# Moving the own part of a token mix into the attention weights, and normalisations to GpSimd, in a one-core perceiver layer

## The reference, cut to what matters

```python
# 1: keys through a cosine of a second projection; softmax; values
K_hat = jnp.cos(jnp.einsum('bsd,dr->bsr', K, Wr) + br)
scores = jnp.einsum('bqr,bkr->bqk', Q, K_hat)
# 2: each token attends to the 8 most similar earlier tokens of its row
attn = jax.nn.softmax(score - row_max, axis=-1)
msg = jnp.einsum('bts,bsd->btd', attn, x)
blended = mix * x + (1.0 - mix) * msg
delta = jax.nn.gelu(blended * gain + bias, approximate=False) * scale
# 3: one of 8 experts (256 -> 1024 -> 256, Gelu) for each token
out = p_max * next_states
```

## Time and profile before

| | us |
|---|---|
| median of 3 runs | 482.03 (481.74 to 483.29) |
| the profiled execution, its own time | 479.15 |
| its span in the trace | 477.3 |

### The profile page before, as it was taken

One profiled execution on the slowest core, in us unless ns is written; L12 is line 12 of the kernel. 1 busy time (PEld: TensorE's weight loads), 2 busy tenths in 40 slices (PEclk: granted clock), 3 DMA queues, 4 the chain that ended last, 5 costly groups with the idle time before them and its releaser, 6 DMA issues. The chain is left out here.

```text
span 477.3 us, 10300 instructions
## 1 busy us (share of the span) xinstructions
PE 420.0 (88%) x3121; PEld 286.7 (60%) x3121; DVE 275.9 (58%) x856; ACT 257.5 (54%) x573; POOL 216.4 (45%) x358
## 2 busy tenths in 40 slices
PE   6767999999969969979877879968999999999992
PEld 6424454445425425434433456857999999999991
DVE  2536887989878868968969946755321221222220
ACT  1455777788847848848756755526232232332330
POOL 1663552765575566556646445364233232222110
PEclk9797999999999989989989989989999999999997
DMA  9996696896775766758776452455679546556100
GB/s 193 309 297 173 153 229 174 222 200 169 194 190 145 197 173 164 224 123 204 227 168 190 167 209 71 162 175 203 209 249 346 186 176 225 172 199 231 33 0 0
DMA packets 119433, 87.45 MB, mean 183 GB/s; under 512 B 78606, under 2 KB 109072, under 8 KB 119252
## 3 DMA queue, kind: packets, MB, share of 16 engines
q1 hardware_dynamic: 111828, 75.82, 56.8%
q0 software_dynamic: 3744, 9.46, 5.7%
q10 hardware_dynamic: 3808, 1.52, 1.5%
HBM read 79.15 MB, written 8.53 MB: 184 GB/s over the span
## 5 line engine op out<-in xcount | busy, mean ns | idle before, releaser
L1206 ACT ACTIVATE XF<-pT,b_now 128x128 f32<-128x128 f32 x184 | 52.2, 369 | 91.0 <-PE pT L1407 91.0
L1407 PEld LDWEIGHTS pT<-XF,stage 128*128 128x128 f32 x736 | 87.8, 195 | 3.9 <-issue 1.7
L1407 PE MATMUL pT<-XF,stage 128*128 128x128 f32 x736 | 89.4, 280 | 0.7 <-issue 0.4
L1420 PE MATMUL pK<-W,XF 128*128 x368 | 85.0, 381 | 2.8 <-ACT XF L1206 2.1
L1420 PEld LDWEIGHTS pK<-W,XF 128*128 128x128 f32 x368 | 67.5, 190 | 11.8 <-issue 3.7
L1382 PE MATMUL pK<-stage,Wkr 128*128 128x512 f32 x128 | 67.7, 656 | 0.0
L305 POOL TENSOR_SCALAR ve<-mv 128x1 f32<-128x1 f32 x48 | 10.9, 227 | 115.1 <-DVE mv L640 115.0
L1382 PE MATMUL pT<-stage,Wkr 128*128 128x512 f32 x128 | 61.6, 605 | 0.0
L1179 ACT ACTIVATE stage<-stage 128x512 f32<-128x512 f32 x64 | 38.7, 627 | 26.1 <-DVE stage L721 26.0
L721 DVE TENSOR_TENSOR stage<-stage 128x512 f32<-128x512 f32 x64 | 49.5, 774 | 0.8
L402 POOL DMA_INDIRECT out_dram<-XF,token_i x23 | 23.1, 1004 | 56.5 <-DVE XF L847 50.4
(11 more groups left out here) (190 smaller groups left out, 679.5 us busy)
## 6 DMA issues: line engine op xcount, KB each, us to landing
stage<-in_L_ffn_W_dram SPq DMA_DIRECT2D x23, 1024.0 KB, 5.1
stage<-in_ctx_dram SPq DMA_DIRECT2D x32, 512.0 KB, 5.1
XF<-in_ctx_dram SPq DMA_DIRECT2D x252, 64.0 KB, 2.3
W<-in_L_ffn_W_dram SPq DMA_DIRECT2D x8, 1024.0 KB, 6.1
rows_by_token<-rows_out SPq DMA_DIRECT2D x16, 256.5 KB
ctx_last<-in_ctx_dram SPq DMA_DIRECT2D x64, 32.0 KB, 4.5
X<-in_x_dram SPq DMA_DIRECT2D x1, 1792.0 KB, 12.6
tokens_by_expert<-no_token POOLq DMA_DIRECT2D x2, 576.0 KB, 8.1
```

The source lines that it names most:

```text
L1206: ins = act.activation(f_hT[b][:, n * P:(n + 1) * P], pT[i][:, (n % 4) * P:(n % 4 + 1) * P], ACT.Gelu, bias=b1_now[:, b, n:n + 1])
L1407: mm = pe.matmul(pT[i][:, (n % 4) * P:(n % 4 + 1) * P], W1[q][:, c, n * P:(n + 1) * P], f_inT[:, q % 2, c * P:(c + 1) * P], start=c == 0, ...
L1420: mm = pe.matmul(p_out, f_hT[q % 2][:, n * P:(n + 1) * P], W2[:, bass.ds(e, 1), n, :].rearrange("p o d -> p (o d)"), start=n == 0, stop=n ...
```

## The change

Own part: the matrix own_part, mix on the diagonal, is made once. A new GpSimd step `mix` forms (1 - mix) * att + own_part from the 128x32 weights, and this is transposed and multiplied with hm = h * gain + bias (rows of the weights sum to one, so the bias may stand inside). The product is blended * gain + bias itself: hg, y and VectorE's addition are gone, and ScalarE takes the Gelu from PSUM.

Normalisations: h and the normalised result are made by GpSimd. `rstd` also makes the negative mean, and the three normalisations are (x + minus_mean) * rstd.

Order: `xn_T` comes after `scores`, its output moves to bank b6; `h_T` comes after a second projection and `probs_T`; `scatter` is split in two in a step, one half in the middle and one at the end; the planning, the second projection's steps and the drain are in another order; the prologue starts with a projection, and the loads that aren't needed early (most of X, the empty token lists) go later. The new `p_rank` and one message use bank b4.

```diff
+        own_part = sb("own_part", [P, T])
...
-        p_xnT = b5[:, 0:D]
+        p_xnT = b6[:, 0:D]
...
-            def rstd(g, mv, ve, rs, mv_r, ve_r, rs_r):
...
+            def rstd(g, mv, ve, minus_mean, rs, i):
...
+                pool.tensor_scalar(minus_mean[:], mv[:, 0:1], -1.0, None, ALU.mult).then_inc(S[f"mean{i}_r"], 1)
...
+            def normal_h(g):
+                at_least(pool, S["hT_tr"], g - 1)
+                at_least(pool, S["hm_m"], g - 1)
+                pool.wait_ge(S["mean2_r"], g + 1)
+                pool.wait_ge(S["rs2_r"], g + 1)
+                pool.tensor_scalar(h[:, g % 2, :], group_of(X, g), minus_mean2[:, 0:1], rs2[:, 0:1], ALU.add, ALU.mult
+                                   ).then_inc(S["h_r"], 1)
...
+            def mix(g):
+                pool.wait_ge(S["att_r"], g + 1)
+                at_least(pool, S["attT_cp"], g)
+                pool.tensor_scalar(mixed[:], att[:], sc[:, 3:4], None, ALU.mult).then_inc(S["others_r"], 1)
+                pool.wait_ge(S["others_r"], g + 1)
+                pool.tensor_tensor(mixed[:], mixed[:], own_part[:], ALU.add).then_inc(S["mixed_r"], 1)
...
+            for s in range(1, NG):
                 if s >= 2:
                     rstd_h(s - 2)
                     base(s - 2)
...
+                    normal_h(s - 2)
+                if s == 3:
+                    own_parts()
+                if s >= 3:
+                    mix(s - 3)
+                last_key(s)
+                last_value(s - 1)
+                if s >= 2:
+                    messages(s - 2)
+                if s == NG - 1:
+                    gather(0)
+                if s >= 6:
+                    if s % 2 == 0:
+                        count_pair(s // 2 - 3)
+                        tokens_of(s // 2 - 3)
+                    else:
+                        scatter(s // 2 - 3, (0,) if s + 1 < NG else (0, 1))
                 if s >= 4:
                     rstd_out(s - 4)
...
+                    rstd_x(s + 1)
                     normal_x(s + 1)
                     add_bv(s + 1)
...
+                if s in (2, 3):
+                    no_tokens(s - 2)
+                if s >= 7 and s % 2 and s + 1 < NG:
+                    scatter(s // 2 - 3, (1,))
...
+            sp.wait_ge(S["ctxT_r"], 2)
+            load_by_feature(1, 1)
...
+            sp.dma_start(X[:, 2:4, :], x_v[:, 2:4, :]).then_inc(S["xnext_ld"], 16)
...
-                act.activation(gel[:], y[:], ACT.Gelu).then_inc(S["gelu_r"], 1)
+                act.activation(gel[:], p_msg[g], ACT.Gelu).then_inc(S["gelu_r"], 1)
...
             def xn_T(g):
                 pe.wait_ge(S["xn_r"], g + 1)
-                at_least(pe, S["selected"], g - 2)
-                at_least(pe, S["y_r"], g - 3)
...
+                at_least(pe, S["x1_r"], g - 1)
...
+            for s in range(1, NG):
                 ctx_project(s, 0, 0)
...
+                scores(s - 1)
                 if s >= 7 and s % 2:
                     pe.wait_ge(S["logits_r"], s - 4)
                     rank(s // 2 - 3)
+                xn_T(s)
+                ctx_project(s, 0, 1)
+                probs_T(s - 1)
                 if s >= 2:
                     h_T(s - 2)
...
+                ctx_project(s, 1, 0)
                 if s >= 2:
...
+                    similar(s - 2)
+                values(s - 1, max(0, (s - 5) // 2))
                 queries(s)
...
+                ctx_project(s, 1, 1)
                 if s >= 2:
                     small_scores(s - 2)
...
+                value_T(s - 1)
```

More of the change, by code:

```diff
@@ L213, in perceiver_layer @@
         p_scoreB = b5[:, 0:T]
-        p_msg = b5[:, 0:D]
+        p_msg = [(b4 if g == NG - 2 else b5)[:, 0:D] for g in range(NG)]
         p_hT = b6[:, 0:D]
@@ L364, in late_constants, with own_parts, tokens_of @@
                 made_at["masks"] = n[0]
-                pool.wait_ge(S["gains"], 2)
-            def scatter(q):
+            def own_parts():
+                made(pool.memset(own_part[:], 0.0))
+                for j in range(BG):
+                    keep(own_part[j * T:(j + 1) * T, :], [[-1, T]], 0, 1, ALU.not_equal, 1.0)
+                pool.wait_ge(S["scal_dve"], 3)
+                made(pool.tensor_scalar(own_part[:], own_part[:], sc[:, 2:3], None, ALU.mult))
+            def tokens_of(q):
                 r0, i = 2 * (q % 2), q % 2
@@ L454, in _ @@
                     add_bv(s + 1)
-                if s >= 2:
-                    self_part(s - 2)
-                if s == 0:
-                    late_constants()
-                if s == NG - 1:
-                    gather(0)
-                if s >= 7 and s % 2:
-                    scatter(s // 2 - 3)
+                if s in (2, 3):
+                    no_tokens(s - 2)
+                if s >= 7 and s % 2 and s + 1 < NG:
+                    scatter(s // 2 - 3, (1,))
+            base(14)
@@ L464, in _ @@
             rstd_h(14)
-            base(14)
-            self_part(14)
+            normal_h(14)
             last_value(15)
-            rstd_out(12)
             gather(1)
             count_pair(5)
+            mix(13)
+            tokens_of(5)
+            gather(2)
+            rstd_out(12)
+            scatter(5)
             rstd_h(15)
             base(15)
-            self_part(15)
-            gather(2)
+            normal_h(15)
+            mix(14)
+            messages(14)
+            rstd_out(13)
@@ L1129, in late_block @@
                 result(j, q, turn)
-            for j in range(4, EARLY):
-                begin(j + 1)
-                end(j)
             for j in range(EARLY, NBLK):
@@ L1250, in xn3T_copy @@
                 act.copy(xn3T[:].rearrange("p c n -> p (c n)"), p_xn3T).then_inc(S["xn3T_cp"], 1)
-            for s in range(NG):
-                xnT_copy(s)
+            turn(0, 0)
+            turn(0, 1)
+            xnT_copy(0)
+            sine(0, 0, 0)
+            sine(0, 0, 1)
+            turn(0, 2)
+            queries(0)
+            act.wait_ge(S["last_fr"], 1)
+            act.activation(khat_last[:], last_frac, ACT.Sin, scale=TWO_PI).then_inc(S["khat_last_r"], 1)
+            turn(0, 3)
+            sine(0, 0, 2)
+            sine(0, 0, 3)
+            for s in range(1, NG):
                 if s >= 3:
@@ L1561, in router @@
                 mm.then_inc(S["route_mm"], 1)
-            for s in range(NG):
-                if s == 0:
-                    last_transposes()
-                xn_T(s)
+            ctx_project(0, 0, 0)
+            ctx_project(0, 0, 1)
+            xn_T(0)
+            last_transposes()
+            ctx_project(0, 1, 0)
+            last_project()
+            small_transposes()
+            queries(0)
+            ctx_project(0, 1, 1)
+            for s in range(1, NG):
                 ctx_project(s, 0, 0)
-                if s == 0:
-                    last_project()
-                if s >= 1:
-                    scores(s - 1)
+                scores(s - 1)
                 if s >= 7 and s % 2:
```

596 lines of the change are left out of this document (301 added, 295 removed).

## The result

The changed kernel takes 447.34 us in the median of four runs (446.76 to 449.0), the kernel before, beside it, 482.66 (481.74 to 483.33): ratio 0.9275, 95% interval 0.9243 to 0.9306. The forecast was 445, with 434 to 461 as its range. The profiled execution took 447.48 us, 31.7 less than the 479.15 of before. The one of before lay 2.9 us under its median and this one doesn't, so the two profiles show some 3 us less of a gain than the medians do.

The account below looks back on a forecast made before the run. TensorE's work and gaps set the end (busy 420.0 of 477.3 us). Gains 5 + 0.7 + 21.6 + 9.5 = 36.8 take the profiled 479.15 to 442.4, the median from 482.03 to 445; range 434 to 461.

Parts of the forecast that it names:

- the drain: Loop's end to block 7's transposes: 77.0 us becomes 67.5, a gain of 9.5, between 3 and 13.
- steps 2 and 3: Second and third loop steps: gain their two short gaps, 0.7 us; X's load in step 2 could cost up to 2.
- the last blocks: Last 16 blocks, from block 7's transposes at 350.25: no TensorE idle time, 7.25 us each; the change touches nothing.
- the loop: Steps 4 to 15: 198.3 us becomes 176.7, 12 steps of 14.6 plus 1.5 for planning; gain 21.6.
- the prologue: Before step 2: group 1's second-half transpose starts at 30, not 35.66; gain 5 us, between 2 and 8.
- The stall, and h_T's place: Even steps from 8: 3.22 us stall and slow projection go; h at 5.0 us, `h_T` at 5.2 instead of 3.1.
- About 14.3 us of TensorE work: Ordinary loop step: 14.90 us stretch with one 0.6 gap; 14.3 of work plus 0.3 of small stalls gives 14.6.
- GpSimd's load: Per loop step: net +1.5 us, +2.8 at the upper price; 12 to 13.3 of 14.3 with `scatter`, so it fits.
- Rival A: GpSimd becomes the loop's bound at normalisations' upper price: step 15.9 us, loop 192, time 459; chance 0.15.
- Interference: More GpSimd instructions slow VectorE's 128x512 subtraction: 0.8 us a step taken, at most 1.7; VectorE then 12.8 of 14.3.
- Gelu from PSUM: ScalarE in each step: Gelu 0.416 before, no cost as work is the same size; if late, `similar` would wait.
- Rival C: Slower than now: bank b6 makes TensorE wait twice a step, 1.3 us each; step 18.5, time 491; chance 0.04.

Follow-up runs that it names:

- first profile: Profiled execution of the changed kernel as first measured, unedited, against the kernel before: 447.48 us, median 447.34, ratio 0.9275.
- its second: Profile from a repeat of the changed kernel, unedited: median 448.64 us over six runs, ratio 0.9284; this profile is 3.7 us longer than the first.

## Why the prediction was right, step by step

**The time: nearer than its parts.** The forecast was made for the profiled execution, 479.15 less 36.8, or 442.4, and moved up to 445 for the median. The profiled execution took 447.48, so the parts brought 32.1 of 36.8 us: the drain is 3.7 short, steps 2 and 3 0.9, the last blocks 0.8, and the loop and the prologue are 0.7 ahead. The median came within 2.3 us because the kernel before had been profiled 3 us under its median and the changed one was not; that much is luck.

**The stall, and h_T's place: right.** The 3.22 us and the slow projection came from `scatter` ahead of `rstd_h`: taking it away alone brought 15 us. In the changed kernel the stall is gone by h_T's later place and a shorter queue ahead of `rstd_h` together. Step 10 starts at 153.55; h is ready 4.0 us into it, where my layout had 5.0, and h_T comes 5.1 us into it, where it had 5.2. GpSimd had more free time than I gave it.

**The work in a step: mis-sized.** "About 14.3 us of TensorE work" was 13.97. I had taken a stretch of 14.90 us and subtracted the 0.6 that its one bracketed gap shows. But its matmuls are 14.18, so it holds 0.72 of idle time: another 0.11 lies ahead of h (92.74 to 92.85), too short for a bracket. And 14.18 is still 0.21 more than the path needs. Step 4, with the 0.6 gap alone, lasts 14.69 (74.92 to 89.61), so this gap costs 0.72. The experiment with `scatter` moved says the same: its steps have shown gaps of 0.2 to 0.4 each and last 14.7. A matmul's shown duration reaches over the start of the next, back to back (1.98 for a projection whose successor starts 1.92 later, 139.55 to 141.47); ahead of a gap this tail is work on the page and lost time on the path. With the 0.3 of "small stalls" that are not there either, the eleven steps are 6.9 us shorter than forecast.

**Step 15: missed.** I gave steps 13 to 15 1.5 us for planning on VectorE and nothing for a wait of GpSimd. Step 15 holds a gap of 4.63 us and 2 us of matmuls at the lower clock behind it. The row of TensorE's gap and the queue of GpSimd above show the cause; the diff showed it beforehand. `gather(0)` stood ahead of `scatter` and `rstd_out`, and I had costed only when its own rows would land, not what is queued behind the waiting instruction. The experiment that puts `rstd_out` first takes the gap away; of its 4.63 us, 2.00 come back as the wait for block 0's rows. These two errors, -6.9 and +6.4, cancel: the loop's total, 176.2 for 176.7, is right by luck.

**GpSimd's load: right in kind, the price 0.24 too high at most.** I took 0.81 us for a normalisation; they take 0.57, 0.59 and 0.77. Its load from step 4 to 14 is 122.0 us in 153.6, or 11.1 a step, where I had 12 to 13.3. Rival A didn't come, but the run with the old form shows that it stood 0.66 us per instruction away, and that its price is 18 to 19.5 us, not the 14 of the rival (459 less 445).

The Trainium skill, "GPSIMD Engine Reference", section 4.1, puts GpSimd at about half of VectorE's speed for operations with two inputs and near it for one input, which these are; the prediction had applied the half. The runs fit neither: (add, mult) takes 0.585 for h on GpSimd where VectorE, with (subtract, mult), takes 0.421, a factor of 1.4; (subtract, mult) takes 1.247 on GpSimd, a factor of 3. The form decides, not the engine alone.

**Interference: none added.** I added 0.8 us a step. VectorE's work is 12.05 us a step (132.52 in eleven), where I had 12.8, and 13.2 less the 1.2 that left it is 12.0 already. Its 128x512 subtraction takes 0.721 in the mean where it took 0.774 before. The rule of the Trainium skill, "SBUF — State Buffer", section "Who interferes with whom", would let more GpSimd work block VectorE more; here 20.0 us more of GpSimd's work (236.4 for 216.4) went with a shorter subtraction. The load as such is not what decides: with the old form of the normalisations GpSimd worked 270.1 us and the subtraction took 0.718, with `scatter` whole 235.3 us and 0.772. Which instructions fall beside each other may decide; no run separates that.

**Gelu from PSUM: right.** 0.384 instead of 0.416, and no wait of TensorE for it. Rival C did not come: from step 4 to the loop's end ScalarE releases one gap of TensorE in the first profile, 0.54 in step 15.

**Steps 2 and 3: 0.2 more instead of 0.7 less.** Their two gaps ahead of h are gone, but in step 2 TensorE now waits 0.62 us for ScalarE's probabilities and 0.48 for o_T.

**The prologue: right in size, not in its path.** Group 1's transpose came at 27.39 and not at 30. The gain was then limited by `last_key(0)` behind the wait for weights, which I hadn't followed, and behind it by ScalarE's probabilities, which the run with the key first shows.

**The drain: 5.8 for 9.5, within its bounds.** TensorE no longer waits for the rows of block 0, which are there by the end of step 15 (246.07), drawn out as it is by its own gap; `rank(5)` and block 3 are as forecast. Not foreseen was the 2.91 gap ahead of `message(15)`, with a slow `down` behind it (3.10 for 1.99). The new stall of 1.5 ahead of block 7 wasn't there: from `rank(7)` at 299.32 the rows are gathered at 310.51, and the transposes at 317.34 follow `down(6)` without a gap. That is 2.9 and 1.1 more and 1.5 less. The other 1.2 of the 3.7 that are missing lie in gaps under 1 us: 0.70, 0.64, 0.82, 0.44, 0.79, 0.58 and 0.94 on the timeline, 4.9, for which I had 3.6 with block 0's 1.

**The last blocks: "the change touches nothing in that" was wrong by 0.8 us** in one profile and 1.7 in the other. The gathers' wait for stores decides there now and then; without it the stretch is 126.99, the 127.05 of before. Why it decides in the changed kernel and not before, and whether the stores land later because of the weights' stream, wasn't measured.

**What no run separates.** The own part in the weights, and with it the Gelu from PSUM, was never run by itself. 15 of the 35 us came with the own part left on VectorE, by an order alone; the rest of the loop's gain, from 14.7 to 13.97 us a step, comes with the own part, h on GpSimd and the new order together. What the own part itself is worth is open.

**Sums that don't come out.** If a step is 14.3 the loop gains 26.7, not 26; TensorE's own work in the drain is 62.6, not 62.4; rival A's loop is 12 x 15.9 = 191, not 192; and the best and worst ends together give 434 and 464, not 433 and 467. None of this moves the forecast by more than 0.2 us.

## What to carry to other kernels

A gap's cure is sought on the engine that releases it, in what is queued ahead of the releasing instruction; and each wait put into an in-order queue is costed by what stands behind it, once for every place where the same helper is called, the irregular last step above all. Two gaps in line with each other hide one another's gain: `xn_T`'s move and `mix(15)`'s each gave nothing alone, the waits for h and for `rank(6)`'s counts taking their place. The total of an engine's waits is not their price; what they delay on the busiest engine is. Read a step's length from start to start of the same instruction, and not as stretch less idle time.

## What the runs showed of the hardware

GpSimd's tensor_scalar over 128x256 fp32 with two per-partition scalars costs 1.25 us as (subtract, mult) for h and 0.585 as (add, mult), in the mean of 16. An indirect DMA occupies GpSimd for about 1.0 us, up to 1.5 in the changed kernel, with 0.3 between two. The store of a block's rows landed in 4.2 us in the median of the changed kernel's first profile (2.0 to 9.0) and in 2.6 in its second (2.0 to 8.1); one that was issued at 315.96 in the first released its waiter only at 322.96.

TensorE behind 4.63 us of idle time ran the next 4 us at the lower of its clocks: the four matmuls of `value_project` took 2.08 us where they take 1.13 else, and the window from the last matmuls before the gap to the step's end has a mean granted clock of 0.66:

```profile
237.04:246.07 9.03, 4.40 (x32) 2.17 (x32) 2.17 (x7) 3.85 (x8) 4.22 (x8) 0.66 0.40 137
```
